# Attention and deformable convolution in one block, in groups of four images

## What is computed

```
x = x + attention(gn(x))           # layer 2: 8 heads of 8, softmax over 256 places, projection
x = x + deformable_conv(gn(x))     # layer 3: 3x3
# layer 3, for input g = gn(x):
offset, mask = conv3x3(g, off_w) + off_b, sigmoid(conv3x3(g, mask_w) + mask_b)
# each of 9 taps samples g bilinearly at its place + tap + offset, times mask
out = sum over 9 taps and 64 channels of weight * sample + bias
```

## Time and profile before

| | |
|---|---|
| three runs | 527.64 us (525.78 to 527.82) |
| span of the profiled execution | 528.0 us; its time outside the span is not shown |
| busy: TensorE, its weight loads, VectorE, ScalarE, GpSimd | 439.1, 231.3, 342.4, 288.9, 132.8 us |
| attention, first scores to last addition | 233.0 to 347.2 us |
| first product of the sampling, last addition | 383.6, 522.8 us |

### The profile page before, as it was taken

The page is one execution under the profiler, slowest core; times in us unless marked ns, Lnnn a source line. Parts: engine busy times, 40 slices in busy tenths (PEclk is TensorE's granted clock), DMA queues, the critical chain, the costliest instruction groups (busy, mean ns, idle before and its releaser), DMA issues. The chain is left out here.

```text
span 528.0 us, 9368 instructions
## 1 busy us (share of the span) xinstructions
PE 439.1 (83%) x3406; PEld 231.3 (44%) x3406; DVE 342.4 (65%) x668; ACT 288.9 (55%) x511; POOL 132.8 (25%) x162
## 2 busy tenths in 40 slices
PE   0527768899999887679999999939898999999995
PEld 0216648555455664223333333324443454454442
DVE  4549876233344568978999996251654778777784
ACT  1279955131532437047878778722865578486441
POOL 4420004000000005744422212031364428065000
PEclk9956997999999988559999999957977999999999
DMA  5500000900000004952200000016390480933302
GB/s 142 164 0 1 0 0 1 197 1 1 0 1 0 1 0 107 279 175 67 73 27 3 3 2 4 0 47 160 100 226 15 89 181 2 217 55 68 67 2 79
DMA packets 20767, 33.79 MB, mean 64 GB/s; under 512 B 5657, under 2 KB 15497, under 8 KB 19957
## 3 DMA queue, kind: packets, MB, share of 16 engines
q1 hardware_dynamic: 16724, 23.70, 18.9%
q0 software_dynamic: 2176, 6.35, 4.3%
q10 hardware_dynamic: 1824, 3.19, 2.3%
HBM read 16.21 MB, written 4.64 MB: 39 GB/s over the span
## 5 line engine op out<-in xcount | busy, mean ns | idle before, releaser
L1335 DVE TENSOR_TENSOR L_s<-L_row_ps,L_cols 128x1024 f32<-128x1024 f32 x72 | 87.6, 1218 | 9.3 <-PE L_row_ps L1500 7.5
L910 DVE TENSOR_REDUCE L_mx<-L_ring 128x2 f32<-128x512 f32 x128 | 83.3, 686 | 12.4 <-PE L_ring L1034 11.8
L965 ACT ACTIVATE L_e<-L_ring 128x512 f32<-128x512 f32 x128 | 73.7, 597 | 21.4 <-PE L_ring L1047 19.3
L1523 PE MATMUL L_acc<-L_s,L_t_sb 128*64 128x256 f32 x576 | 81.6, 406 | 1.1 <-DVE L_s L1335 1.0
L1404 ACT ACTIVATE L_cols<-L_col_ps 128x512 f32<-128x512 f32 x72 | 42.8, 596 | 48.9 <-PE L_col_ps L1510 48.5
L1034 PE MATMUL L_ring<-stacks_k_st,stacks_q_st 64*128 64x256 bf16 x256 | 51.0, 301 | 7.0 <-DMA stacks_k_st<-L_k_parts 4.7
L1523 PEld LDWEIGHTS L_acc<-L_s,L_t_sb 128*64 128x64 f32 x576 | 36.0, 140 | 35.9 <-DVE L_s L1335 19.8
L1047 PE MATMUL L_ring<-stacks_q_st,stacks_k_st 64*128 64x256 bf16 x256 | 47.2, 282 | 1.2 <-DMA stacks_q_st<-L_m_parts 1.2
L1500 PE MATMUL L_row_ps<-L_hats,L_sel 48*128 48x512 bf16 x144 | 44.6, 392 | 0.0
L1067 PE MATMUL L_ctx_ps<-L_e,L_v_x 128*32 128x256 f32 x512 | 41.5, 398 | 0.0
L1311 DVE COPY L_t_sb<-L_acc 128x192 f32<-128x192 f32 x48 | 17.1, 357 | 31.4 <-PE L_acc L1491 31.4
(11 more groups left out here) (270 smaller groups left out, 814.2 us busy)
## 6 DMA issues: line engine op xcount, KB each, us to landing
L_hats<-L_parts SPq DMA_DIRECT2D x28, 216.0 KB, 5.0
L_hat<-L_offsets SPq DMA_DIRECT2D x20, 192.0 KB, 4.7
L_mask<-L_offsets SPq DMA_DIRECT2D x10, 192.0 KB, 4.9
stacks_q_st<-L_q_parts SPq DMA_DIRECT2D x12, 128.0 KB, 3.9
stacks_k_st<-L_k_parts ACTq DMA_DIRECT2D x12, 128.0 KB, 4.8
stacks_q_st<-L_q_parts POOLq DMA_DIRECT2D x12, 128.0 KB, 2.7
stacks_k_st<-L_k_parts POOLq DMA_DIRECT2D x12, 128.0 KB, 2.9
L_stack<-L_xpad SPq DMA_DIRECT2D x7, 162.0 KB, 5.8
```

What stands on the lines that cost most here:

```text
L910: dve.tensor_reduce(mx[:, n % 2, :, head], ring[:, place(step) % 3].rearrange("p (q s) -> p q s", q=2), AX.X, ALU.max).then_inc(max_read, 1)
L965: act.activation(e[:, k], ring[:, 3 + v % 3], ACT.Exp, scale=HD2 ** -0.5).then_inc(e_ready, 1)
L1335: dve.tensor_tensor(s[:, q], row_ps[:, q], cols[:, t % 3:t % 3 + 1].broadcast_to([P, 2, 2 * N]), ALU.mult).then_inc(s_ready, 1)
L1523: mm = pe.matmul(acc[C * e:C * e + C, b, 0:N], t_sb[:, b, h, (KK * e + t) * C:(KK * e + t + 1) * C], s[:, q, h, e * N:(e + 1) * N], start= ...
```

## The change

`layer2` and `layer3` become one function and one block, `layers2and3`. What the third layer did ahead of its sampling moves into the rows of the attention, in groups of four images:

- VectorE's statistics of a pair stay per channel; `norm_stats(g)` exchanges neighbouring partitions (`stream_shuffle`) and aggregates, in rows 44, 76, 108 and 140. GpSimd makes scale and shift (`norm_x`, with a power instead of square root and reciprocal), pads (`pad_x`) and normalizes the first pair. `xpad` has four pairs, `stack` eight images.
- The first group's convolution stands in row 58 in one go, on a bank of the ring of maxima; the second's pieces in rows 112 to 118, the third's in rows 128 to 134, the fourth's in the second pair's first tap. The mask is `0.5 * tanh(0.5 a) + 0.5`: tanh on ScalarE, the rest on GpSimd (`gate`).
- Offsets and masks of a group go out in two copies and come back in three (64 partitions of 9 KB each). `to_places` and the spreads by TensorE are gone.
- The first chunk's hats are made by ScalarE in rows 82 to 92, weighed by GpSimd, split by VectorE in rows 109 to 120. `weigh_first` weighs the first pair in rows 114 to 124; the first rows and columns are spread in row 134, the first product stands in row 136.
- SyncE's queue takes, between the maxima of the images, stacks, offsets and places; its loop is written out. PSUM is one tensor of eight banks; the third layer's tiles lie over the attention's in SBUF.

The core of the diff:

```diff
+    FIRST_OFFSETS = 58
+    OFFSETS = (None, 112, 128)
+    FIRST_HATS, FIRST_SPLIT, FIRST_WEIGHTS, FIRST_SPREAD = 82, 109, 114, 134
+    LAST_OFFSETS = (1, 0)
...
+                def send_stack(g):
+                    sp.wait_ge(edge_ready, 2)
+                    sp.wait_ge(xpad_ready, 2 * g + 2)
+                    if g > 1:
+                        sp.wait_ge(off_conv, g - 1)
+                    src = xpad[:, 2 * (g % 2):2 * (g % 2) + 2, :]
+                    dst = stack[:, CH * (g % 2):CH * (g % 2) + CH, :].rearrange("p (n e) s -> p n e s", e=2)
+                    for half in range(2):
+                        sp.dma_start(dst[0:C, :, half, :], src[C * half:C * half + C]).then_inc(stack_in[g], 16)
+                        sp.dma_start(dst[C:P, :, half, 0:(HP - 1) * WP], src[C * half:C * half + C, :, WP:HP * WP]).then_inc(stack_in[g], 16)
...
+                for n in range(B):
+                    send_maxima(n)
+                    if n == 7:
+                        send_stack(0)
+                    if n == 8:
+                        store_offsets(0)
+                    if n == 9:
+                        load_places(0)
+                    if n == 11:
+                        send_stack(1)
+                send_stack(2)
+                store_offsets(1)
+                send_hats(0, 0)
+                send_hats(0, 1)
+                load_places(1)
+                store_offsets(2)
+                send_stack(3)
+                load_places(2)
...
+                def norm_x(g):
+                    two = slice(2 * g, 2 * g + 2)
+                    pool.wait_ge(mv_ready, 2 * g + 2)
+                    step(pool.tensor_scalar(var[:, two], mv[:, two, 1], 1.0, EPS, ALU.mult, ALU.add))
+                    step(pool.tensor_tensor(scale[:, two], var[:, two], minus_half[:], ALU.pow))
+                    step(pool.tensor_scalar(shift[:, two], mv[:, two, 0], -1.0, 0.0, ALU.mult, ALU.add))
+                    pool.tensor_tensor(shift[:, two], shift[:, two], scale[:, two], ALU.mult).then_inc(normed, 1)
...
+                    if n == 6:
+                        pool.wait_ge(s_ready, 32)
+                        pool.memset(xpad[:], 0.0).then_inc(edge_ready, 1)
+                        pool.wait_ge(edge_ready, 2)
+                        norm_x(0)
+                        pad_x(0)
...
+                    if n == 8:
+                        gate(0)
+                    if n == 10:
+                        norm_x(1)
+                        pad_x(1)
+                    if 11 <= n < 14:
+                        weigh_hat(pool, 0, n - 11)
+                    if n == 14:
+                        norm_x(2)
+                        pad_x(2)
...
+                def split_hat(j, part):
+                    if part == 0:
+                        dve.wait_ge(masked, j + 1)
+                        own(dve.tensor_copy(parts3[:, 0, third(j)], hat[:, 0, third(j)]))
+                    if part == 1:
+                        if j > 1:
+                            dve.wait_ge(parts3_ready, j - 1)
+                        own(dve.tensor_tensor(rest3[:, j % 2], hat[:, 0, third(j)], parts3[:, 0, third(j)], ALU.subtract))
+                    if part == 2:
+                        own(dve.tensor_copy(parts3[:, 1, third(j)], rest3[:, j % 2]))
+                    if part == 3:
+                        dve.tensor_tensor(parts3[:, 2, third(j)], rest3[:, j % 2], parts3[:, 1, third(j)], ALU.subtract).then_inc(parts3_ready, 1)
...
+                    if v % 32 == 12 and v > 12:
+                        norm_stats(v // 32 - 1)
+                    if 0 <= v - FIRST_SPLIT < 12:
+                        split_hat(*divmod(v - FIRST_SPLIT, 4))
+                    if v - FIRST_WEIGHTS in range(1, 13, 2):
+                        take_first_weighed((v - FIRST_WEIGHTS) // 2, 0)
+                        take_first_weighed((v - FIRST_WEIGHTS) // 2, 1)
+                    if v == FIRST_SPREAD + 2:
+                        sample(0, 0)
...
+                def take_offsets(g, out):
+                    if g > 1:
+                        act.wait_ge(off_stored, 32 * (g - 1))
+                    act.activation(off[:, g % 2], out, ACT.Identity, bias=vec3[:, 0:1]).then_inc(off_ready, 1)
+                    act.wait_ge(off_ready, g + 1)
+                    act.activation(sig[:, g % 2], off[:, g % 2], ACT.Tanh, scale=0.5).then_inc(tanh_ready, 1)
...
+                    if v == FIRST_OFFSETS:
+                        bank_free(("offsets", 0))
+                        for piece in range(7):
+                            conv_offsets(0, ring[:, place["offsets", 0] % 3, 0:N], piece)
+                    if v == OFFSETS[1]:
+                        pe.wait_ge(m_read, B)
+                    for g in range(1, 3):
+                        if 0 <= v - OFFSETS[g] < 7:
+                            if g == 2 and v == OFFSETS[g]:
+                                pe.wait_ge(off_ready, g)
+                            conv_offsets(g, ring[:, 0, 0:N], v - OFFSETS[g])
+                    if v - FIRST_WEIGHTS in range(0, 12, 2):
+                        weigh_first((v - FIRST_WEIGHTS) // 2)
+                    if v == FIRST_SPREAD:
+                        pe.wait_ge(sel_ready, 1)
+                        pe.wait_ge(e_ready, 8 * B)
+                        pe.wait_ge(first_read, 12)
+                        spread_cols(0)
+                        spread_rows(0)
+                        spread_cols(1)
+                pe.wait_ge(o_added, B)
+                pe.wait_ge(off_ready, 3)
...
+                        if (n, t) == LAST_OFFSETS:
+                            at = col_at["offsets", 3]
+                            pe.wait_ge(col_read, at - 1)
+                            for piece in range(7):
+                                conv_offsets(3, col_ps[:, at % 2, 0:N], piece, col_ready)
```

More of the change, by code:

```diff
@@ new lines, in send_hats @@
+                def send_hats(c, b):
+                    sp.wait_ge(parts3_ready, 3 * c + 3)
+                    if c:
+                        sp.wait_ge(product_used, KK * (2 * (c - 1) + b) + 10)
+                    else:
+                        sp.wait_ge(s_ready, 96)
+                    for k in range(2):
+                        for half in range(2):
+                            first = C * k + 2 * b + half
+                            sp.dma_start(hats[C * k:C * k + 3 * H, b, half], parts3[first:C * k + C:CH]).then_inc(hats_in[b], 16)
@@ L958, in _ @@
                 act.wait_ge(parts_ready, 2 * NQ)
+                weights.wait(act, 3)
                 def exponents(v):
@@ new lines, in weigh_first @@
+                def weigh_first(k):
+                    if k == 0:
+                        pe.wait_ge(xn3_ready, 1)
+                    else:
+                        pe.wait_ge(first_read, 2 * k)
+                    for half in range(2):
+                        rows = slice(C * half, C * half + C)
+                        pe.matmul(ring[:, 1 + half, 0:TW], xn3[rows, 0, k // 3 * P:(k // 3 + 1) * P], w_all[rows, k % 3 * TW:(k % 3 + 1) * TW],
+                                  start=True, stop=True).then_inc(first_ready, 1)
@@ new lines, in samples @@
+                def samples(n, b, t):
+                    u, q = KK * n + t, (b + t) % 2
+                    pe.wait_ge(product_ready, u + 3)
+                    if t == 0:
+                        pe.wait_ge(added, n + 1)
+                        if n:
+                            pe.wait_ge(col_read, col_at["weighed", 6 * n + 5] + 1)
+                        pe.wait_ge(first_read, 6 * n + 12)
+                    for h in range(2):
+                        for half in range(2):
+                            mm = pe.matmul(acc[C * half:C * half + C, b, 0:N], t_sb[b][:, h, (KK * half + t) * C:(KK * half + t + 1) * C],
+                                           products[:, q, h, half * N:(half + 1) * N], start=(t == 0 and h == 0), stop=(t == KK - 1 and h == 1))
+                    mm.then_inc(product_used, 1)
@@ L1558, in _ @@
+                        v = KK * n + t
                         if v + 1 < KK * NP:
```

741 lines of the change are left out of this document (313 added, 428 removed).

## The result

The changed kernel took 509.31 us in the median of four runs (503.65 to 513.51), the kernel before beside it 526.71 (525.52 to 527.82): a ratio of 0.958, 95% interval 0.954 to 0.963. Forecast were 508.0, between 497 and 518. Run again later beside other kernels, it took 510.71 (509.02 to 511.79; ratio 0.971, 0.967 to 0.976).

The account below looks back on a forecast made before the run. TensorE bounds the attention; before sampling, a preamble without samples and a first pair waiting for hats. Terms -44.6 + 1.9 + 7.1 + 3.0 + 9.1 + 2.2 + 1.2 + 0.2 = -19.9 from 528.0, less 0.36: 508 us, range 497 to 518.

Parts of the forecast that it names:

- the preamble and the first pair: From the attention's last addition to the second pair: 60.2 us replaced by 15.6, so -44.6.
- the last rows: Rows 128 to 134: the third group's seven convolution pieces cost +3.0 us, between 1.5 and 6.
- the third pair on: Sampling from the third pair onward: nothing changes.
- ScalarE's hats: Rows 82 to 92: six ScalarE operations, partly taken up by banks of scores, cost 1.2 us, bounds 0 and 3.6.
- table load beside the tanh: ScalarE's tanh in the attention: taken as 0, with up to 7.7 us of table loads kept in the range.
- Row 58: First group's convolution, 3.04 us, with TensorE waiting 2.7 for the stack, then half clock: +9.1 us in all.
- Maxima behind bulk: Rows 56, 80, 88 and 96: maxima queue on SyncE with stacks, offsets and places, +2.2 us, bounds 0 and 7.
- Rows 111 to 127: Second group's convolution and six weighings on TensorE, hats split on VectorE: +7.1 us, between 5 and 10.
- Second pair: The fourth group's convolution in its first step covers 1.4 us of waiting for hats: 19.3 us, +1.9.
- Costed at nothing: Places of images 4 to 7 land about when sampling starts: free, but up to 4 us if late.
- the inputs are there in time: Rival: the stack lands before 282, so row 58's wait, its clock and late maxima go: 498 us, chance 0.22.
- the dear queue: Rival: the queue costs more, by a second clock drop, late hats or crowded VectorE: 518 us, chance 0.16.
- The clock that stays low: Rival: close waits from row 58 to 96 keep half clock up to row 112: 551 us, chance 0.03.

Follow-up runs that it names:

- row 66: Changed kernel with the first group's convolution, and what hangs on it, one image later, in row 66 and not 58: 504.14 us, ratio 0.957.
- after's profile: Profile of the changed kernel's shortest execution, unedited: span 501.85 us against 528.0 for the kernel before.
- the fourth experiment: Changed kernel with VectorE taking the first chunk's weighed copies ahead of the row's addition, not behind it: 507.03 us, ratio 0.960.
- the fourth convolution: Changed kernel with the fourth group's convolution in the second pair's fifth step, not its first: 511.66 us, ratio 0.965.
- the order of the places: Changed kernel with SyncE loading the places of images 4 to 7 ahead of the second pair's hats: 506.85 us, ratio 0.961.
- the filler: Changed kernel with TensorE multiplying a constant matrix eight times while it waits at row 58: 509.05 us, ratio 0.967.

## Why the prediction was right

**Right, and the bulk of the gain:** the preamble and the first pair, -44.8 against -44.6; the last rows, +3.1 by taking the convolution out, against +3.0; nothing from the third pair on; the attention longer by 19.4 us (133.0 from row 0 to the last addition, for 113.6), within the 13 to 35 named; ScalarE's hats, 0.9 in rows 80 to 88 against 1.2 (in row 66's kernel, which makes the hats eight rows later, rows 80 to 88 take 6.74 for before's 6.69); and no table load beside the tanh, so that term is 0. By the Trainium skill, "ScalarE: Activation LUTs", section "Table sets: the hidden batching unit", tanh shares a set with exp; the trace agrees, as it has no load behind the early one at the start of the block.

**Row 58: the mechanism right, the price too high** (9.1; measured 4.8, or 6.5 with the clock). The stack landed 3.0 us after row 57's exponent (279.84 - 276.83), not 4.5 (285.2 - 280.73): GpSimd's six operations took 2.7 (267.42 to 270.13) for 2.4, the stack's four copies 5.0 (274.82 to 279.84) for 5.1, but what stood ahead of the copies delayed them 1.4 less than I had summed. TensorE idled 1.75 us (forecast 2.7). The half-clock stretch behind it was 3.4 us long, not the 6.83 of the earlier trace rows, so it costs 1.7, in five profiles of eight.

**Maxima behind bulk:** +1.4 and +1.2 at row 80 in the two profiles (forecast 1.0), of which 1.0 and 0.9 go with the places out of SyncE's queue. The maxima did land behind the places, as said, but they do so from another queue as well: what I had not seen is that SyncE's wait for the maxima of image 9 delays the bulk. Nothing at rows 56, 88 and 96, where I had put 1.2.

**Rows 111 to 127, the step that failed in its reason:** "each copy is waited for by the next weighing: 0.3". TensorE's own addition is 5.7 (18.34 - 12.68), not 6.8, as pieces fill gaps; but copies stood behind additions in VectorE's order, which cost 2.4, and 2.9 with the clock. VectorE had the time, as I said, and the wrong order. The upper end that I kept was summed wrongly: a split of 28 us with the copies, statistics and additions beside it makes some 37 on VectorE, 15 over TensorE's 21.6 and not 7. It didn't come.

**Second pair:** +3.4 for 1.9. I let the convolution cover the wait for hats; it delays the hats on ScalarE as much as TensorE. At the fifth step it is +2.2.

**Last rows:** +3.9 and +3.7 for 3.0, with 2.2 and 1.8 us at half clock, where I had counted on a full one; 9.62 at full clock is +2.9.

**Costed at nothing:** the places of images 4 to 7. Named as up to 4 us if late, they made ScalarE wait 1.0 us in after's profile, at no cost to TensorE, and 4.2 in the fourth experiment's, which cost TensorE 3.1.

So the median was met by a sum in which row 58 and the maxima were about 3 to 5 us too dear and rows 111 to 127, the last rows and the second pair about 4 too cheap: that it came out so close is in part luck, and runs of one and the same code lay between 503.65 and 513.51. Of the rivals, "the inputs are there in time" is what row 66 makes of the kernel, 504 and not 498, since the wait and its clock were smaller. Of the dear queue one part came true in most profiles, a second drop of the clock near the start of the sampling: ten of the twelve profiles of changed kernels had one between row 120 and the end of the first pair, 3.4 to 13.7 us at half clock in sum. The clock that stays low never came: behind row 57 it fell for 3.4 or 6.8 us at a time. The first pair's hats were in time by 7.0 us (landed 352.20, spread at 359.24), for the 6 said.

## What to carry to other kernels

When two stages are laid over each other, price the order on each engine's queue, not only its busy time: three gains here (row 66, the copies, the fourth convolution) were reorderings that remove no work; with the order of the places, which shows no gain by itself, they took 9 to 10 us. Ask of each wait which instruction stands ahead of the one waited for, and whether that one waits too. Idle time of an engine is not room for work: the third convolution cost its full 3.1 us in the last rows, where TensorE idles 2 us with or without it, and moved into a pair where TensorE is hardly ever idle it cost nearly as much.

## What was not expected of the hardware

GpSimd paid for sharing time with VectorE, and VectorE hardly did. The same two paddings of 256 columns took 1.10 us beside reductions from the ring and 2.88 beside casts and subtractions of hats, and so, within 0.02, in all twelve profiles of changed kernels:

```profile
269.08 1.10 POOL L1003 TENSOR_SCALAR L_xpad<-all_x,L_scale,L_shift 128x256 f32<-128x256 f32 x2
...
332.67 2.88 POOL L1003 TENSOR_SCALAR L_xpad<-all_x,L_scale,L_shift 128x256 f32<-128x256 f32 x2
```

VectorE's subtraction took 1.12 at the worst there, 0.95 otherwise, and its casts 0.55, where the forecast kept 1.26 for a smaller one in mind; there it was VectorE that lost. The Trainium skill, "GPSIMD Engine Reference", section 8 "Key points", has the two colliding; the trace agrees, with GpSimd as the one that lost most here.

And one idle time of 1.75 us had two outcomes, full clock or half, in executions of one and the same code; what decides between them no run here shows. Nor do the runs show that it makes the spread: the changed kernel's lay within 9.9 us the first time and within 2.8 the second, the filler's within 4.7, those without the wait within 1.9 to 3.0.
